# Experts' down projection as five float32r products, a quarter of the first product in fp32, SiLU on ScalarE, and three shared blocks left for the end

## What is computed

```python
scores = softmax(xf @ gate_w.T)                      # 64 experts, top 6 kept
gx = xp[buf_tok]                                     # 64 x 128 rows of 512
gu = einsum('ech,ehi->eci', gx, gate_up_proj)        # 512 -> 384 = gate 192, up 192
g, u = split(gu, 2, axis=-1)
hid = silu(g) * u                                    # 128 x 192
eo = einsum('eci,eih->ech', hid, down_proj) * buf_w  # 192 -> 512, scaled by the router's weight
routed = zeros((T + 1, h)).at[buf_tok].add(eo)
shared = silu(xf @ shared_gate_w.T) * (xf @ shared_up_w.T) @ shared_down_w.T   # 512 -> 384 -> 512
x = layernorm(x + routed + shared)
```

## Time and profile before

| | us |
|---|---|
| median of 3 runs | 948.13 (943.59 to 950.84) |
| span of the profiled execution | 945.2 |
| PE busy | 918.1 (97%) |
| DVE busy | 683.3 (72%) |
| ACT busy | 499.5 (53%) |
| POOL busy | 460.9 (49%) |

### The profile page before, as it was taken

One profiled execution on the slowest core, in us unless ns is written; L12 is line 12 of the kernel. 1 busy time (PEld: TensorE's weight loads), 2 busy tenths in 40 slices (PEclk: granted clock), 3 DMA queues, 4 the chain that ended last, 5 costly groups with the idle time before them and its releaser, 6 DMA issues. The chain is left out here.

```text
span 945.2 us, 15175 instructions
## 1 busy us (share of the span) xinstructions
PE 918.1 (97%) x4626; PEld 727.5 (77%) x4626; DVE 683.3 (72%) x1250; ACT 499.5 (53%) x1015; POOL 460.9 (49%) x540
## 2 busy tenths in 40 slices
PE   9999999999999999998999999999999999999996
PEld 7788888888888888776787777777777677767875
DVE  7996878879797877987766666665655565636776
ACT  5543434344443535453456665666555566545775
POOL 2002456665656656677135445554545544433564
PEclk9999999999999999999999999999999999999998
DMA  7244735434342516275569999999999999969972
GB/s 209 89 155 121 176 90 158 117 108 132 125 127 75 177 59 204 79 268 173 174 196 302 308 322 322 321 316 318 322 287 307 305 305 303 322 113 392 382 259 111
DMA packets 114190, 203.91 MB, mean 216 GB/s; under 512 B 18496, under 2 KB 56384, under 8 KB 113088
## 3 DMA queue, kind: packets, MB, share of 16 engines
q1 hardware_dynamic: 93584, 159.87, 51.6%
q0 software_dynamic: 19520, 35.75, 16.7%
q10 hardware_dynamic: 1008, 7.34, 2.2%
HBM read 143.03 MB, written 59.88 MB: 215 GB/s over the span
## 5 line engine op out<-in xcount | busy, mean ns | idle before, releaser
L1535 POOL DMA_INDIRECT slot_table<-tokens,slot_of x162 | 181.0, 1118 | 86.7 <-issue 50.3
L1577 POOL DMA_INDIRECT acc_rows<-eo,table_sb x64 | 110.6, 1729 | 172.5 <-ACT eo L888 127.2
L1632 PE MATMUL bank<-x_hi,wqkv_hi 128*128 128x512 f32 x384 | 152.1, 396 | 0.3 <-DVE wqkv_lo L972 0.3
L1632 PE MATMUL bank<-x_hi,wqkv_lo 128*128 128x512 f32 x384 | 150.2, 391 | 0.0
L1632 PE MATMUL bank<-x_lo,wqkv_hi 128*128 128x512 f32 x384 | 150.2, 391 | 0.0
L1404 DVE TENSOR_TENSOR wgu_lo<-wgu,wgu_hi 128x1536 fp32r<-128x1536 f32 x64 | 112.4, 1758 | 48.0 <-ACT wgu_hi L882 48.0
L1632 PE MATMUL bank<-wdn,hid_et 96*128 96x512 f32 x256 | 122.8, 602 | 8.2 <-ACT hid_et L924 8.2
L882 ACT CAST wgu_hi<-wgu 128x1536 fp32r<-128x1536 f32 x64 | 94.5, 1477 | 5.8 <-DMA wgu<-w_gu 5.4
L1566 POOL DMA_INDIRECT xg<-x_rows,table_sb x64 | 74.3, 1162 | 41.3 <-DVE table_sb L1133 22.0
L1632 PE MATMUL bank<-wgu_hi,xgt_hi 128*128 128x384 f32 x256 | 91.4, 357 | 0.0
L1632 PE MATMUL bank<-wgu_hi,xgt_lo 128*128 128x384 f32 x256 | 85.9, 335 | 0.0
(11 more groups left out here) (183 smaller groups left out, 2146.0 us busy)
## 6 DMA issues: line engine op xcount, KB each, us to landing
wgu<-w_gu SPq DMA_DIRECT2D x64, 768.0 KB, 8.5
wdn<-w_down SPq DMA_DIRECT2D x64, 384.0 KB, 8.5
xres<-x SPq DMA_DIRECT2D x32, 256.0 KB, 2.9
x_turned<-x1t SPq DMA_DIRECT2D x32, 256.0 KB
x_rows<-x SPq DMA_DIRECT2D x32, 256.0 KB, 3.0
acc_rows<-x SPq DMA_DIRECT2D x32, 256.0 KB, 3.1
fin<-acc_rows SPq DMA_DIRECT2D x8, 1024.0 KB, 12.1
odd<-acc_rows SPq DMA_DIRECT2D x8, 1024.0 KB, 13.9
```

What stands on the lines that cost most here:

```text
L1535: pool.indirect_dma_start(table_dram, bass.IndirectOffsetOnAxis(slot_of[:, i, k:k + 1], 0), tokens[:, i:i + 1], None, bounds_check=SLOTS - ...
L1577: pool.indirect_dma_start(acc_dram[e % 2], bass.IndirectOffsetOnAxis(table_sb[:, e:e + 1], 0), eo[eo_slot[e]][:, :], None, bounds_check=T ...
L1632: mm = pe.matmul(out_ap, a, b, start=first and i == 0, stop=final and i == len(products) - 1)
```

## The change

- **Down projection.** The 192 rows of its weights now lie as 128 partitions of 768: the first 128 rows with all 512 columns, and the other 64 rows folded, columns 0 to 255 on partitions 0 to 63 and 256 to 511 on 64 to 127. ACT makes `wdn_hi` (128x512) and the high halves of `wdn_mix` (two copies of 64x256), DVE makes `wdn_lo` and fills the other halves of `wdn_mix` with low parts (two of 64x256, to the other 64 partitions). The hidden rows are written 256 wide, their last 64 columns twice, so that the turned tile holds them on both halves; ACT makes `het_hi`, DVE `het_lo` of it. The product is five float32r matmuls of 512 columns: `three` on the first 128 rows, and `wdn_mix` with het_hi and with het_lo.
- **First product.** Chunks 0 to 2 stay in three products each; chunk 3 is one plain fp32 product from `xgt_full` and the loaded weights. ACT and DVE split 384 columns of rows and 1152 of weights instead of 512 and 1536; ACT copies the last 128 columns of the rows.
- **SiLU.** `silu_e` is one ACTIVATE Silu on ACT and no longer an operation of DVE; the same for `silu_s` from the shared expert's block 1 on.
- **Blocks.** `TAIL` = 3: 29 units stand in the loop, 22 in the tail. 20 early tiles and 12 in pairs are finished there; two early tiles follow each of the units 14 to 19. `odd` has four buffers instead of five, the down weights four instead of three.

```diff
-    TAIL = 4
+    TAIL = 3
-    NG, ND, NXG, AHEAD = 4, 3, 6, 4
+    NG, ND, NXG, AHEAD = 4, 4, 6, 4
...
-    NFA, NFB = 6, 5
+    NFA, NFB = 6, 4
...
-    EARLY_AFTER = {**{i: 1 for i in range(8, 14)}, **{i: 1 for i in range(16, 22)}, **{i: 1 for i in range(24, 28)}}
+    EARLY_AFTER = {**{i: 1 for i in range(8, 14)}, **{i: 2 for i in range(14, 20)}, **{i: 1 for i in range(20, 22)}}
...
@@ scalar
-                        act.activation(tanh_s[:, :], ps[:, :], ACT.Tanh, scale=0.5).then_inc(tanh_done, 1)
+                        if b:
+                            act.wait_ge(hid_s_done, n)
+                            act.activation(silu_s[:, :], ps[:, :], ACT.Silu).then_inc(silu_done, 1)
...
+            def split_down_of(e):
+                act.wait_ge(dn_in[e % ND], 16 * (e // ND + 1))
+                if e >= 2:
+                    act.wait_ge(eo_mm, e - 1)
+                w, mix = wdn_buf[e % ND], wdn_mix[e % 2]
+                act.copy(wdn_hi[e % 2][:, :], w[:, 0:D])
+                act.copy(mix[0:IB, 0:DH], w[0:IB, D:DN])
+                act.copy(mix[IB:P, DH:D], w[IB:P, D:DN]).then_inc(wdn_hi_done, 1)
...
-                    act.wait_ge(silu_e_done, e)
-                act.activation(tanh_e[:, :], gu_ps[e % 2][:, 0:I], ACT.Tanh, scale=0.5).then_inc(tanh_e_done, 1)
+                    act.wait_ge(hid_e_done, e)
+                act.activation(silu_e[:, :], gu_ps[e % 2][:, 0:I], ACT.Silu).then_inc(silu_e_done, 1)
...
-                act.copy(hid_et[e % 2][:, :, :], ht_ps[0:IH, 0:2 * P].rearrange("p (h s) -> p h s", h=2)).then_inc(hid_et_done, 1)
+                act.copy(het_hi[e % 2][:, :, :], ht_ps[:, 0:2 * P].rearrange("p (h s) -> p h s", h=2)).then_inc(het_hi_done, 1)
+                if e + 1 < NE:
+                    split_down_of(e + 1)
@@ vector
+            def split_down_of(e):
+                dve.wait_ge(wdn_hi_done, e + 1)
+                w, mix = wdn_buf[e % ND], wdn_mix[e % 2]
+                dve.tensor_tensor(wdn_lo[e % ND][:, :], w[:, 0:D], wdn_hi[e % 2][:, :].bitcast(F32), ALU.subtract)
+                dve.tensor_tensor(mix[IB:P, 0:DH], w[0:IB, D:DN], mix[0:IB, 0:DH].bitcast(F32), ALU.subtract)
+                dve.tensor_tensor(mix[0:IB, DH:D], w[IB:P, D:DN], mix[IB:P, DH:D].bitcast(F32), ALU.subtract).then_inc(wdn_lo_done, 1)
...
-                dve.scalar_tensor_tensor(out=hid_e[e % 2][:, :], in0=silu_e[:, :], scalar=0.5, in1=ps[:, I:GU],
-                                         op0=ALU.mult, op1=ALU.mult).then_inc(hid_e_done, 1)
+                dve.tensor_tensor(hid_e[e % 2][:, 0:I], silu_e[:, :], ps[:, I:GU], ALU.mult)
+                dve.tensor_tensor(hid_e[e % 2][:, I:2 * P], silu_e[:, P:I], ps[:, I + P:GU], ALU.mult).then_inc(hid_e_done, 1)
...
+                turned_low(e)
+                if e + 1 < NE:
+                    split_down_of(e + 1)
@@ tensor
-                pe.wait_ge(hid_et_done, e + 1)
-                pe.wait_ge(dn_in[e % ND], 16 * (e // ND + 1))
+                pe.wait_ge(het_lo_done, e + 1)
+                pe.wait_ge(wdn_lo_done, e + 1)
...
-                chain(eo_ps[:, :], [(hid_et[e % 2][:, k, :], wdn_buf[e % ND][:, k, :]) for k in range(2)]).then_inc(eo_mm, 1)
+                products = three(het_hi[e % 2][:, 0, :], het_lo[e % 2][:, 0, :], wdn_hi[e % 2][:, :], wdn_lo[e % ND][:, :])
+                products += [(part[e % 2][:, 1, :], wdn_mix[e % 2][:, :]) for part in (het_hi, het_lo)]
+                chain(eo_ps[:, :], products).then_inc(eo_mm, 1)
...
-                for k in range(KC):
+                for k in range(KS):
                     products += three(xgt_hi[e % 2][:, k, :], xgt_lo[e % 2][:, k, :], wgu_hi[e % 2][:, k, :], wgu_lo[e % NG][:, k, :])
+                for k in range(KS, KC):
+                    products.append((xgt_full[e % 2][:, k - KS, :], wgu_buf[e % NG][:, k, :]))
```

More of the change, by code:

```diff
@@ L89, in build @@
     wgu_buf = [both.place(f"wgu{i}", [P, KC, GU]) for i in range(2)]
-    wdn_buf = [both.place(f"wdn{i}", [IH, 2, D]) for i in range(2)]
+    wdn_at = [both.at + 4 * i * DN for i in range(2)]
+    wdn_buf = [both.place(f"wdn{i}", [P, DN]) for i in range(2)]
     att = Map(nc, both.at, end)
@@ L206, in build @@
     xg = [late.place(f"xg{i}", [P, D + E]) for i in range(NXG - 2)]
-    xgt_hi = [late.place(f"xgt_hi{i}", [P, KC, P], F32R) for i in range(2)]
-    xgt_lo = [late.place(f"xgt_lo{i}", [P, KC, P], F32R) for i in range(2)]
+    xgt_hi = [late.place(f"xgt_hi{i}", [P, KS, P], F32R) for i in range(2)]
+    xgt_lo = [late.place(f"xgt_lo{i}", [P, KS, P], F32R) for i in range(2)]
+    xgt_full = [late.place(f"xgt_full{i}", [P, KC - KS, P]) for i in range(2)]
     eo = [Map(nc, x_at + 2 * half - 4 * D, x_at + 2 * half).place("eo0", [P, D]),
@@ L211, in build @@
           Map(nc, x_at + 4 * half - 4 * D, x_at + 4 * half).place("eo2", [P, D])]
-    tanh_e = late.place("tanh_e", [P, I])
     silu_e = late.place("silu_e", [P, I])
-    hid_e = [late.place(f"hid_e{i}", [P, I]) for i in range(2)]
-    hid_et = [late.place(f"hid_et{i}", [IH, 2, P]) for i in range(2)]
+    hid_e = [late.place(f"hid_e{i}", [P, 2 * P]) for i in range(2)]
+    het_hi = [late.place(f"het_hi{i}", [P, 2, P], F32R) for i in range(2)]
+    het_lo = [late.place(f"het_lo{i}", [P, 2, P], F32R) for i in range(2)]
     assert late.at <= kept_from
     late.end = end
-    wgu_hi = [late.place(f"wgu_hi{i}", [P, KC, GU], F32R) for i in range(2)]
+    wgu_hi = [late.place(f"wgu_hi{i}", [P, KS, GU], F32R) for i in range(2)]
+    wdn_hi = [late.place(f"wdn_hi{i}", [P, D], F32R) for i in range(2)]
+    wdn_mix = [late.place(f"wdn_mix{i}", [P, D], F32R) for i in range(2)]
     xg += [late.place(f"xg{i}", [P, D + E]) for i in range(NXG - 2, NXG)]
-    fin_map = Map(nc, both.at - 2 * 4 * (KC * GU + 2 * D), both.at)
+    fin_map = Map(nc, both.at - 2 * 4 * (KC * GU + DN), both.at)
     fin_sb = [fin_map.place(f"fin{i}", [P, NJ, D]) for i in range(2)]
-    NFA, NFB = 6, 5
+    NFA, NFB = 6, 4
     fin_map = Map(nc, projected_end, projected_end + 8 * 4 * BT)
@@ L552, in _ @@
                 load_gate_up(e)
-            for e in range(2, ND):
+            load_down(2)
+            sp.wait_ge(heads_mm, NB)
+            for e in range(3, ND):
                 load_down(e)
@@ L1230, in unit @@
                     ps = proj_ps[(unit_take(b) + part) % 3]
-                    if part % 2 == 0:
+                    if part % 2 == 0 and b == 0:
                         dve.wait_ge(tanh_done, n + 1)
@@ L1242, in unit @@
                             dve.wait_ge(hid_lo_done, n)
-                        dve.scalar_tensor_tensor(out=hid_s[:, :], in0=silu_s[:, :], scalar=0.5, in1=ps[:, :],
+                        dve.scalar_tensor_tensor(out=hid_s[:, :], in0=silu_s[:, :], scalar=1.0 if b else 0.5, in1=ps[:, :],
                                                  op0=ALU.mult, op1=ALU.mult).then_inc(hid_s_done, 1)
@@ L1895, in _ @@
                 if e:
-                    pe.wait_ge(hid_et_done, e)
-                for k in range(2):
-                    mm = pe.transpose(ht_ps[0:IH, k * P:(k + 1) * P], hid_e[e % 2][:, k * IH:(k + 1) * IH], ident[:, :])
+                    pe.wait_ge(het_lo_done, e)
+                for h in range(2):
+                    mm = pe.transpose(ht_ps[:, h * P:(h + 1) * P], hid_e[e % 2][:, h * P:(h + 1) * P], ident[:, :])
                 mm.then_inc(ht_mm, 1)
@@ L1916 @@
     gu, down = a["L0_ffn_gate_up_proj"], a["L0_ffn_down_proj"]
-    experts, inner = gu.shape[0], down.shape[1] // 2
+    experts, half = gu.shape[0], D // 2
     gu = gu.reshape(experts, D // P, P, -1).transpose(0, 2, 1, 3)
-    down = down.reshape(experts, 2, inner, D).transpose(0, 2, 1, 3)
+    rest = down[:, P:].reshape(experts, -1, 2, half).transpose(0, 2, 1, 3).reshape(experts, P, half)
+    down = np.concatenate([down[:, :P], rest], axis=2)
     decay = np.repeat(a["L0_attn_decay_param"], D // HEADS).reshape(D // P, P).T
```

57 lines of the change are left out of this document (35 added, 22 removed).

## The result

The changed kernel takes 961.9 us (median of 4 runs, 958.6 to 962.5) beside 948.8 for the kernel before: ratio 1.015, interval 1.011 to 1.020. It is slower by 13 us, or 1.5%. The profiled execution's span is 960.7 (before: 945.2).

What follows compares the result with a forecast made beforehand. PE was taken to bound loop and tail, with new loop stalls from ACT and DVE. Span 945.2, +20 in the loop, -13 in the tail: 952; the median lies 2.9 above, so 955 us, range 922 to 974.

Steps and rivals of the forecast that it cites:

- the forecast case: Whole kernel: most likely 955 us, own range 942 to 966 with stalls of 15 to 33 us; chance 50%.
- my 4.09 + 2.72: PE in the loop: 4.09 us of steps per expert instead of 4.46, plus 2.72 for a gate or up unit.
- seven counted on each engine: Loop, per expert: seven overlaps of successive instructions, 0.1 us each on ACT (sum 4.0), 0.08 on DVE (sum 3.85).
- The loop, +20: Loop: 351 of PE's steps + 26 new stalls + 6 old losses = 383 us, against 363.4.
- the walk: Loop: PE, ACT and DVE followed step by step behind an up unit; hid_e done at 4.74, new stalls 26 us altogether.
- the 6 us of old losses that I kept: Loop: of the 12.7 us it lost before, 6 stay, since longer experts leave the queues more room; bounds 0 and 12.7.
- PE "idle for about 30": Loop, sign of being right: PE idle for about 30 us of some 383, put down to DVE's hid_e and xgt_lo.
- The tail, -13: Tail: 103.8 less 24.5 of PE's steps, plus 8.7 and 3 us, gives 91.
- DVE's backlog, +8.7: Tail, units 14 to 21: DVE has 33 us of work beside PE's 24.5, falls 8.7 behind and holds PE back.
- "DVE over 90% busy": Tail, sign of being right: DVE over 90% busy in the middle of the tail, and the tail near 91 us.
- "Hand-overs cost more.": Rival, loop: waits between ACT and DVE break overlaps; 53 us of stalls instead of 26, total 982, half of it 967; 20%.
- "PE stays the bound": Rival: ACT and DVE keep ahead of PE, the 26 us vanish; total 935, or 924 without DVE's tail backlog; chance 27%.

Runs made afterwards that it cites:

- the run with tanh: Changed kernel with the shared blocks' SiLU again as tanh on ACT and product on DVE, experts keeping Silu: 965.5 us, ratio 1.018.
- two moved groups on DVE: Changed kernel with DVE's low parts of down weights moved behind hid_e and xgt_lo, and wgu_lo behind het_lo: 941.3 us; with 4 blocks left behind too, 929.8.

## Why the prediction was right, and where it was not

I forecast 955, a range of 922 to 974, and most chance on slower. Measured are 961.9, slower by 1.5%: inside the forecast case's own 942 to 966, 7 us above its number. All of the 7 us are the tail's.

- *PE's steps.* Down steps are 0.23 us, and an expert with a unit takes 6.79 to 6.82, my 4.09 + 2.72. A light one takes 4.22 where hid_e does not stall it, of which 0.19 is the wait for xgt_lo: PE's own steps are 4.03, 0.06 below my sum.
- *ACT and DVE's sums.* Every duration taken from a neighbour's row held within 0.03 us on average, the copies of 64 partitions at 0.40 too. ACT was busy for 77% of the loop (75% expected). The overlaps did not hold: of seven counted on each engine three are missing, so ACT needs 4.17 us an expert instead of 4.0 and DVE 4.1 to 4.2 instead of 3.85. (And "before it was 3.4" on ACT is a sum without overlaps; with three, it is 3.1.)
- *The loop, +20.* It came out at +19.6. The mechanism was right: the walk puts the losses in the experts behind units, through the split of the down weights that stands ahead of hid_e on DVE, and moving that work away took them off. The sizes were near: behind an up unit 1.48 each on average instead of 1.15, behind a gate unit 0.70 instead of 0.45, behind a row unit 0.69 instead of 0.85, and 1.8 in all behind light ones instead of 2. Together 30.6 instead of 26. What the walk has too short is DVE's part: it has hid_e done at 4.74, measured are 5.15 (540.59 against 535.44), since the missing overlaps are on the way. And the 6 us of old losses that I kept came out at about 1. That these two errors, +4.6 and -5, cancel to within 0.4 us is luck. (PE "idle for about 30" is 30.6 by its steps; by its busy time, which counts overlapping records once, it is 18.7.)
- *The tail, -13.* It came out at -5.8. The term mis-sized is DVE's backlog, +8.7: the last block's units cost +19.2. I counted DVE's work behind each unit and left out that each tile goes from DVE to POOL, ACT, POOL and ACT again, in queues in which the SiLU of the next unit stands. The 24.5 us of PE's steps were saved and 19.2 of them given back. "DVE over 90% busy" was seen from 902 to 917 us. It is not nothing, as the run with tanh shows (3.7 us), but it is not what the SiLU at 922.70 waited for.
- *Rivals.* "Hand-overs cost more" has its condition fulfilled, an ACT sum of 4.1 up, but not its price: the stalls are 30.6 us, not its 40 to 53, and with the same work on ACT light experts go at 4.22 once DVE's order is changed. "PE stays the bound" is what two moved groups on DVE make of it: 941, and 930 with 4 blocks.
- *Parts of the change.* Down part, fp32 chunk and SiLU together: 0.4% faster. Blocks: 16 to 19 us slower, with or without them.

## What to carry to other kernels

Sums per engine say who could be the bound; when three are within 10% of each other, follow the chain of hand-overs from the last point at which all engines are level, here the end of a unit, to the next place where the first engine waits. When you look for the loss in a trace, sort the repeats by what stood ahead of them and not only by what they hold: by their own kind the light experts were one group of 4.99 us, by their predecessor most of them fall into three, of 5.54, 4.78 and 4.25. In an in-order queue put first what another engine waits for soonest, and work whose result is wanted late (here the low parts of weights) behind it. Work moved out of a tail saves only what the tail's other chains, here the final tiles, let it save.
